# Moving the SBUF buffers of a fused attention and mixture-of-experts kernel to other byte offsets

## The reference

```
x = x + 0.5 * ffn(layernorm(x))       # f = 0 in the kernel
x = x + attention(layernorm(x))
x = x + 0.5 * ffn(layernorm(x))       # f = 1

ffn(z)  = (silu(z @ sg) * (z @ su)) @ sd              # shared expert, width 2048
        + for 8 experts of width 1024, capacity 640:  # top 2 of 8 per row
              w * (silu(zg @ rg) * (zg @ ru)) @ rd    # gathered rows, scattered back with add
attention: groups of 64 rows, 16 heads of 16 channels, RMS-normed q and k, causal softmax, projection
```

## The kernel before

| tensor | before | mod 512 | mod 64 | after | mod 512 | mod 64 |
|---|---|---|---|---|---|---|
| x | 16512 | 128 | 0 | 16896 | 0 | 0 |
| w1 (and raw) | 49280 | 128 | 0 | 49664 | 0 | 0 |
| stage | 98432 | 128 | 0 | 131584 | 0 | 0 |
| empty | 106368 | 384 | 0 | 139520 | 256 | 0 |
| zh | 112320 | 192 | 0 | 98816 | 0 | 0 |
| zl | 120512 | 192 | 0 | 107008 | 0 | 0 |
| hh, hl | 136896, 140992 | 192 | 0 | 123392, 127488 | 0 | 0 |
| zn | 145088 | 192 | 0 | 144960 | 64 | 0 |
| w0, aw | 153568 | 480 | 32 | 153600 | 0 | 0 |
| xr | 202720 | 480 | 32 | 202752 | 0 | 0 |
| azh, azl | 208864, 209888 | 480 | 32 | 208896, 209920 | 0 | 0 |
| k_t, q_t, qcat, kcat, vv, qk, p_s | 169952 to 212960 | 480 | 32 | 169984 to 212992 | 0 | 0 |
| ph, pl | 217120, 221216 | 32 | 32 | 217088, 221184 | 0 | 0 |
| yh, yl, y_s | 226464, 227488, 225440 | 160 | 32 | 226304, 227328, 225280 | 0 | 0 |

## Time and profile before

### The profile page before, as it was taken

How to read it: one execution, slowest core, us unless ns; L and a number is a source line. 1 busy time by engine, 2 the same in 40 slices (tenths; PEclk the granted TensorE clock), 3 DMA queues, 4 the chain that set the end, 5 groups by cost and what they waited for, 6 DMA issues and landing times.

```text
span 2171.5 us, 38386 instructions
## 1 busy us (share of the span) xinstructions
PE 2136.9 (98%) x14227; PEld 1956.4 (90%) x14227; DVE 1429.1 (66%) x3141; ACT 1031.1 (47%) x2006; POOL 461.2 (21%) x439
## 2 busy tenths in 40 slices
PE   8999999999999999999999999999999999999999
PEld 7888899999998888888888888888999999988888
DVE  6666556666665788888898996666466666633333
ACT  3333335554553666666666663333355555522222
POOL 2322211121113222222224322332112121200000
PEclk9999999999999999999999999999999999999999
DMA  9331224554445000000101101321244444441010
GB/s 269 105 106 57 74 62 129 133 143 109 96 108 168 21 1 21 21 20 1 35 1 57 38 11 68 110 79 60 69 104 105 110 100 103 116 128 59 30 59 20
DMA packets 194602, 168.41 MB, mean 78 GB/s; under 512 B 17017, under 2 KB 175149, under 8 KB 194416
## 3 DMA queue, kind: packets, MB, share of 16 engines
q1 hardware_dynamic: 176752, 144.57, 22.2%
q0 software_dynamic: 17664, 21.38, 5.6%
HBM read 104.32 MB, written 68.07 MB: 79 GB/s over the span
## 4 chain that ended last, share of the span: by engine, by line
PE 85%; DVE 8%; issue 3%; SPq 2%; DMA 1%; ACT 1%; POOL 0%; DVEq 0%; ACTq 0%; POOLq 0%
PE gate_up_p L338 28%; PE quad L338 24%; PE out_p L376 21%; PE misc L376 4%; PE misc L508 2%; PE quad L525 2%; DVE p_s L1166 1%; PE misc L402 1%; PE quad L539 1%; SPq L1567 1%; DVE smax L1162 1%; DVE y_s L1177 1%; PE misc L394 1%; PE misc L413 1%; DVE pl L1249 1%
## 5 line engine op out<-in xcount | busy, mean ns | idle before, releaser
L338 PE MATMUL gate_up_p<-zh,w 128*128 128x512 f32 (+2 forms) x2368 | 710.4, 363 | 1.2 <-DVE h_s L1038 1.2
L708 ACT CAST hh<-h_s 128x512 fp32r<-128x512 f32 (+2 forms) x511 | 276.0, 540 | 683.1 <-DVE h_s L1038 680.7
L376 PE MATMUL out_p<-w,hh 128*128 128x256 f32 x2808 | 558.4, 281 | 5.6 <-DVE hl L1054 5.5
L338 PE MATMUL quad<-zh,w 128*128 128x512 f32 (+2 forms) x1728 | 484.3, 348 | 0.0
L338 PEld LDWEIGHTS gate_up_p<-zh,w 128*128 128x128 f32 x2368 | 431.1, 189 | 51.5 <-DVE h_s L1038 2.2
L376 PEld LDWEIGHTS out_p<-w,hh 128*128 128x128 f32 x2808 | 457.0, 189 | 16.2 <-DVE hl L1054 6.9
L338 PE MATMUL gate_up_p<-zl,w 128*128 128x512 f32 (+2 forms) x1184 | 423.6, 358 | 0.0
L376 PE MATMUL out_p<-w,hl 128*128 128x256 f32 x1404 | 393.0, 280 | 0.0
L1038 DVE TENSOR_TENSOR h_s<-gate_up_p,sg_s 128x512 f32<-128x512 f32 (+2 forms) x296 | 178.4, 603 | 255.8 <-PE gate_up_p L338 242.6
L1054 DVE TENSOR_TENSOR hl<-h_s,hh 128x512 fp32r<-128x512 f32 (+2 forms) x431 | 247.2, 573 | 136.1 <-ACT hh L708 120.8
L338 PEld LDWEIGHTS quad<-zh,w 128*128 128x128 f32 x1728 | 309.5, 189 | 27.0
(11 more groups left out here) (200 smaller groups left out, 2796.4 us busy)
## 6 DMA issues: line engine op xcount, KB each, us to landing
stage<-in_L_ffn_rg SPq DMA_DIRECT2D x128, 128.0 KB, 2.7
stage<-in_L_ffn_ru SPq DMA_DIRECT2D x128, 128.0 KB, 3.0
stage<-in_L_ffn_rd SPq DMA_DIRECT2D x128, 128.0 KB, 3.1
slots_d<-empty SPq DMA_DIRECT2D x16, 662.5 KB, 7.1
zh_d<-zh SPq DMA_DIRECT2D x16, 512.0 KB, 3.1
zl_d<-zl SPq DMA_DIRECT2D x16, 512.0 KB, 4.3
y_d<-x SPq DMA_DIRECT2D x16, 512.0 KB, 5.4
zh<-zh_d SPq DMA_DIRECT2D x16, 512.0 KB, 4.2
```

The lines of the kernel that those rows point to most:

```text
L338: last = pe.matmul(dst, a, b, start=(k == 0), stop=(k == 3 * n - 1))
L376: last = pe.matmul(out[:, j // 2, o:o + C], a[:, par, cols], w[:, hi, :], start=(c == 0 and i == 0 and j % 2 == 0), stop=(c == NCH - 1 and ...
L708: nc.scalar.copy(hh[:, n % 2, 0:ncol], h_s[:, n % 2, 0:ncol]).then_inc(sm["hh_done"], 1)
```

## The change

Only the order of the `sb(...)` lines and two unused tensors change; no instruction, wait or size does. `gap0` (384 bytes) comes ahead of `x`; `zh`, `zl`, `sg_s`, `h_s`, `hh`, `hl` move to just behind `w1`; `gap1` (160 bytes) comes ahead of `w0` and the attention's tensors; three small attention tensors move behind the large ones; `itok`, which POOL uses while it builds constants at the start, moves to a place that `w1` covers later.

```
+        sb("gap0", [P, 96], F32)
         x = sb("x", [P, NT, C], F32)
         start_mem = ExitStack()
         raw = sb("raw", [P, NCH, PIECE], F32, start_mem)
+        itok = sb("itok", [P, 4 * NT], I32, start_mem)
         start_mem.close()
         w1 = sb("w1", [P, 2, NCH, PIECE], F32R)
+        zh = sb("zh", [P, 2, KC, SB], F32R)
+        zl = sb("zl", [P, 2, KC, SB], F32R)
+        sg_s = sb("sg_s", [P, 2, SB], F32)
+        h_s = sb("h_s", [P, 2, SB], F32)
+        hh = sb("hh", [P, 2, SB], F32R)
+        hl = sb("hl", [P, 2, SB], F32R)
         stage = sb("stage", [P, 2, PIECE], F32)
...
-        itok = sb("itok", [P, 4 * NT], I32)
...
-        zh = sb("zh", [P, 2, KC, SB], F32R)
-        zl = sb("zl", [P, 2, KC, SB], F32R)
-        sg_s = sb("sg_s", [P, 2, SB], F32)
-        h_s = sb("h_s", [P, 2, SB], F32)
-        hh = sb("hh", [P, 2, SB], F32R)
-        hl = sb("hl", [P, 2, SB], F32R)
         zn = sb("zn", [P, 2, BT, ROW], F32)
 
+        sb("gap1", [P, 40], F32)
         ffn_mem = ExitStack()
         w0 = sb("w0", [P, 2, NCH, PIECE], F32R, ffn_mem)
...
         p_s = sb("p_s", [P, NH, GROUP], F32, att)
-        smax = sb("smax", [P, NH], F32, att)
         ph = sb("ph", [P, NH // 2, P], F32R, att)
         pl = sb("pl", [P, NH // 2, P], F32R, att)
-        den_a = sb("den_a", [P, NH], F32, att)
-        rden = sb("rden", [P, NH], F32, att)
         y_s = sb("y_s", [P, C], F32, att)
         yh = sb("yh", [P, KC, P], F32R, att)
         yl = sb("yl", [P, KC, P], F32R, att)
+        smax = sb("smax", [P, NH], F32, att)
+        den_a = sb("den_a", [P, NH], F32, att)
+        rden = sb("rden", [P, NH], F32, att)
```

## The result

| | median us | lowest to highest | runs |
|---|---|---|---|
| before | 2175.40 | 2168.24 to 2179.18 | 20 |
| after | 2180.86 | 2175.69 to 2186.10 | 20 |

The ratio is 1.0027 with a 95% interval of 1.0020 to 1.0034. The change makes the kernel slower by 0.27%, that is 5.9 us (4.4 to 7.4); the two medians are 5.5 us apart. The forecast was 2162 us and faster; the time lies outside the range of 2148 to 2175. The kernel before has itself moved, from 2172.73 over 3 runs to 2175.40 over 20. The profiled execution after has a span of 2180.5 us, against 2171.5 before.

A forecast was written before the change was run, and what follows sets the result against it. TensorE was taken to bound the ffn phases, DVE and TensorE alternately the fused stage; savings of 3.4 + 3.9 + 2.3 + 1.0 = 10.6 us gave 2162 us, 0.49% less, with a range of 2148 to 2175.

The forecast's parts named there:

- What bounds the kernel: TensorE alone in the ffn phases, some 15 us of DVE work per fused step, one DMA at the start.
- I take the start modulo 64 as the cause: ffn phases: w1 beats w0 by 0.061 us a chunk, 0.29 an expert, because w1 starts on a multiple of 64 bytes.
- The prediction's own sign of being wrong: Forecast wrong if the last phase's chunk isn't below 4.17 us, or the fused stage (678 us) moves over 3 us.
- Items 1 and 2: w0 reaching w1's rate in s0 of ffn 0 saves 3.4 us, in s1 of ffn 1 3.9 us.
- Item 3: w0 reaching w1's rate in the experts, four in each ffn, saves 8 x 0.29 = 2.3 us.
- Item 4: Attention tensors on a multiple of 64 speed up fused-stage matmuls, saving 1.0 us, bounds 0 and 1.7.
- Item 5: w1, zh, zl, hh, hl, x going from 128 or 192 to 0 modulo 512: taken as 0, not shown by the trace.
- Items 6 to 8: DVE, ACT and POOL operands, DMA sides in SBUF, and itok under w1 with the gaps: 0 each.
- item 7: DMA sides in SBUF move to 0 modulo 512; only the start's 4.50 us stall could go or double; taken as 0.
- Same remainder collides: Rival, chance 0.11: operands starting at equal remainders slow each other, w1's stretches lose 7.6 us, giving 2180.3 us.
- Nothing changes: Rival, chance 0.17: start modulo 64 is not the cause, w0 keeps its rate, 2172.7 us.
- Best rate: Rival, chance 0.12: all TensorE reads reach the fastest pace, gate and up 1.36 us throughout; 16 us beyond forecast, 2146.

The follow-up runs named there:

- e2: Kernel before, with only w0 and the attention tensors moved, from 480 to 0 modulo 512: 2177.60 us, ratio 1.0005 to the kernel before.
- e3: Changed kernel with every tensor 32 bytes further, distances unchanged: 2183.59 us, ratio 1.0035 to the kernel before.
- e1: Separate TensorE-only kernel, series of 48 matmuls sweeping the byte distance between operand starts: at 256 columns 120 ns for distance 0, 113.5 for 64.
- e5: Separate TensorE-only kernel running the chunk sequence for 64 pairs of distances (gate and up, down): 512-row chunk 4133 ns at (192, 64), 4180 at (0, 0).
- e7: Changed kernel with zh, zl, hh and hl 64 bytes further, weight buffers unmoved: 2171.59 us, ratio 0.9967 to the kernel before.
- run 384: Not a follow-up run: the words say that the experts work on chunks of 384 and 256 rows; no separate time belongs to them.
- e6: Kernel before with w0 moved from 480 to 128 modulo 512, giving it w1's distances: 2169.94 us, ratio 0.9949 to the kernel before.
- e8: Separate TensorE-only series with 128, 96, 64 or 32 stationary columns: at 256 columns and distance 0, 120.0 ns with 128, 113.3 from 64 down.

## Why the prediction was wrong

- *What bounds the kernel* held. TensorE's start-to-start pace in the ffn phases is the time, and nanoseconds per matmul added up as they were counted. In the fused stage the reading was loose: of the "15 us of DVE work" between 897.13 and 912.55 the chain gives 3.8 us as "issue" and 0.7 to POOL. Nothing in the sum hangs on it.
- *The failing step* is the sentence "I take the start modulo 64 as the cause". e2 and e3 refute it; e1 and e5 to e7 show the distance modulo 256 in its place. The prediction's own sign of being wrong came true: the last phase's chunk is 4.180 us, not below 4.17. w0 and w1 in the kernel before differed in three things at once (start modulo 64, place, distance to z and h), so the "experiment in the trace" could not choose. The one argument against distance was that aw and azh have equal remainders and are slow, as w0 is, which has unequal ones. It assumed that equality alone could matter; 120 ns at d = 0 and 117.8 at d = 224 are two points of one table.
- *Items 1 and 2* (w0 in the shared phases, 3.4 and 3.9 us): 1.0 and 1.3. Gate and up did reach 2.75, for another reason, and down lost most of it again.
- *Item 3* (w0 in the experts, 2.3 us faster): 2.2 slower. The experts run 384 and 256 rows; a chunk of 384 rows at (0, 0) takes 3.15 us, as it did with w0 and w1 before, and one of 256 rows 2.16, the slowest in the table.
- *Item 4* (attention, 1.0 us): 0. aw with azh had d = 0 before and after and stays at 120 ns, a pace that e1 shows for d = 0 at each start tried; yh with aw went from d = 192 to 0 and from 0.71 to 0.73 us, where 0.70 was forecast. The fused stage took 678.2 and 678.3 us.
- *Item 5* (w1, z, h "from one multiple of 64 to another", taken as 0): +1.9 us in `s0` of ffn 1, and 4.6 in the eight experts that read w1. This was where the sign turned: w1 with z and h sat at the best of e5's 64 pairs, and the change took it away.
- *Items 6 to 8*: 0, as forecast. On item 7 the Trainium skill's 256-byte rule ("DMA: Bandwidth & Descriptors", "How a descriptor splits into AXI transactions") would have shortened the stall; it went from 4.50 to 4.64 us, so no run here shows it.
- *The rivals.* "Same remainder collides", given 0.11, had the sign and the place in w1's stretches. That its 2180.3 us meets the measured 2180.86 is luck: it stands for 7.6 us more than before, and 5.9 (4.4 to 7.4) were measured, on top of a kernel before that had moved by 2.7. Its mechanism is right only in part: the sign it named, 2.80 where w1 is read, did not come (2.75); the condition for turning slower, a pair dearer than 4.200 us a chunk, did not come true (4.180); and the fused stage, from which it took 2.4 us, got no longer. The loss sits in the 256-column matmuls, most of it in experts. "Nothing changes", for which the 16-byte lines of the Trainium skill ("SBUF — State Buffer", "Specifications (TRN2)") were named, fails in e1: all starts but those at d = 4 are multiples of 16 and the paces differ. "Best rate" did not come; 1.36 gave way to 1.44.
- *The range* left out the collision on the ground of two rows 1 to 2 ns apart, called hardly outside rounding. With 14,227 matmuls in the kernel, one nanosecond in each would be 14 us. The other ground was a slip: "no slower than w0's 1.42 / 12" is 118.3 ns, and aw with azh take 0.72 / 6 = 120. The pair at equal remainders was the slowest of the 256-column rows that the prediction shows.

## What to carry to other kernels

A difference between two buffers in one trace shows that something differs, not which of their properties; before an address is blamed, list every relation it stands in (itself, and to each partner operand), and time the pair alone over a sweep. In float32r kernels bound by TensorE the distance between stationary and moving start modulo 256 bytes is worth up to 3% at 512 columns and 6% at 256 in single matmuls, and 0.5% of this kernel (e6); choose it by measuring the kernel's own sequence of shapes, with some 32 to 160 bytes of padding as the price. Round addresses for everything make all distances 0, which at 256 columns is among the slowest.

## What the runs showed of the hardware

- Back to back float32r matmuls at full clock with 128 x 128 stationary operands: 226.7 to 234.3 ns at 512 columns, 173.3 or 174.7 at 384, 113.3 to 120.0 at 256, by the distance of the two starts modulo 256 bytes and, at some distances, by what ran before. The Trainium skill ("TensorE: Matmul & The Clock Gate", "Back-to-back issue gap") gives N / 2.4 + 2.5 ns for a matmul by itself, by which an estimate is 216 and 109 ns, and says that in a stream of pairs weight load and matmul set the spacing together. No series here reached the estimate, and e8 agrees with the second statement: at 256 columns and d = 0 the pace falls from 120.0 to 113.3 ns as the stationary columns go from 128 to 64.
- The Trainium skill ("SBUF — State Buffer", "SBUF: two separate sides") says that TensorE never waits on anyone for SBUF. In e1, with no other engine at work and the one copy of data landed, the same matmul takes 113.3 or 120.0 ns by where its two operands lie. So no other engine and no transfer makes the difference. It doesn't contradict that statement, which is about other users of SBUF, and shows that TensorE's pace still depends on where its operands lie.
- The durations of matmuls in the profile (0.28 us in e1) do not show the pace; starts do.
- Open: what the two reads do to each other, why fewer stationary columns are slower at 512 columns and d = 0, which of its paces a series falls into, and what takes up TensorE's slower pace in the fused stage. Not tried: different distances in different phases.
